# A two-layer adaLN block over 16 samples on one core: a new order of calls on every engine

## The reference

```
h = layernorm(x) * (1 + ca) + sa
x = x + ga * attention(h)                 # softmax((q k + q rel) / sqrt(8)) v, 16 heads
h = layernorm(x) * (1 + cb) + sb
x = x + gb * experts(h)                   # top 4 of 16, down((up + 1) * gate * sigmoid(1.702 gate))
# second layer, other weights
h = layernorm(x) * (1 + ca) + sa
k = exp(1j * 10 * (h @ Wk)); v = h @ Wv   # 1024 columns each
pos   = real(cumsum(v * rotors) * conj(rotors)) / sqrt(t)
assoc = real(cumsum(v * conj(shift(k))) * k)    / sqrt(t)
x = x + ga * ((pos * g0 + assoc * g1) @ Wo)
h = layernorm(x) * (1 + cb) + sb
x = x + gb * sigmoid(xr @ Wr) * (relu(xk @ Wk2)**2 @ Wv2)
```

## Time and profile before

| | |
|---|---|
| median of 3 runs | 1395.64 us (1394.96 to 1398.1) |
| the profiled execution, first to last instruction | 1390.0 us |
| mean granted TensorE clock | 0.994 |
| one steady step | 81.3 us |
| busy over the span | PE 90%, DVE 82%, ACT 70%, POOL 20% |
| DMA | 29.8 MB, mean 21 GB/s |

### The profile page before, as it was taken

How to read it: one execution, slowest core, us unless ns; L and a number is a source line. 1 busy time by engine, 2 the same in 40 slices (tenths; PEclk the granted TensorE clock), 3 DMA queues, 4 the chain that set the end, 5 groups by cost and what they waited for, 6 DMA issues and landing times.

```text
span 1390.0 us, 22686 instructions
## 1 busy us (share of the span) xinstructions
PE 1248.1 (90%) x7130; PEld 938.9 (68%) x7130; DVE 1136.3 (82%) x2104; ACT 970.5 (70%) x1699; POOL 280.8 (20%) x258
## 2 busy tenths in 40 slices
PE   7798998989899898989989898998989899898989
PEld 5475775758577575757758575775857577585778
DVE  7758879797987979798797979879797987979765
ACT  1665767778676777867677786767778676776841
POOL 4030221303022130302213031221303122130200
PEclk9899999999999999999999999999999999999999
DMA  5330301204030110403012030301204030120000
GB/s 126 93 35 5 35 9 16 20 8 34 8 34 8 15 19 8 34 8 32 10 13 21 8 34 8 31 10 13 21 8 34 8 31 11 12 22 5 1 4 4
DMA packets 54392, 29.82 MB, mean 21 GB/s; under 512 B 3725, under 2 KB 53338, under 8 KB 54362
## 3 DMA queue, kind: packets, MB, share of 16 engines
q1 hardware_dynamic: 52472, 28.74, 17.2%
q10 hardware_dynamic: 1890, 0.70, 0.5%
HBM read 8.20 MB, written 2.10 MB: 7 GB/s over the span
## 4 chain that ended last, share of the span: by engine, by line
PE 56%; DVE 14%; ACT 14%; issue 10%; POOL 2%; DMA 1%; SPq 1%; ACTq 1%; DVEq 0%; POOLq 0%
PE ring L762 15%; PE pb L862 7%; PE pa L776 7%; DVE smax L1814 5%; PE pa L680 4%; PE ring L667 3%; PE ring L716 3%; PE pb_k L792 2%; DVE prod L1927 2%; ACT prob L1279 2%; PE ring L749 2%; PE ring L629 2%; PE pb_v L820 1%; ACT L1383 1%; ACT frac L1386 1%
## 5 line engine op out<-in xcount | busy, mean ns | idle before, releaser
L427 POOL TENSOR_TENSOR gsc<-gsc,sc_all 128x512 f32<-128x512 f32 x128 | 175.7, 1377 | 353.2 <-ACT gsc L1344 353.2
L762 PE MATMUL ring<-ht,wgu 128*128 128x256 f32 x1024 | 241.5, 384 | 1.0 <-ACT sc_all L1332 1.0
L1954 DVE TENSOR_TENSOR_SCAN prod<-keep,prod 128x512 f32<-128x512 f32 x188 | 224.2, 1214 | 0.0
L762 PEld LDWEIGHTS ring<-ht,wgu 128*128 128x128 f32 x1024 | 193.2, 191 | 34.8 <-issue 5.0
L1814 DVE TENSOR_REDUCE smax<-ring 128x4 f32<-128x1024 f32 x128 | 153.3, 1219 | 17.6 <-PE ring L629 10.8
L1887 DVE SCALAR_TENSOR_TENSOR prob<-prob,gsc 128x512 f32<-128x512 f32 x120 | 81.4, 688 | 81.9 <-POOL gsc L427 63.5
L862 PE MATMUL pb<-prod,wo 128*128 128x256 f32 x544 | 129.3, 382 | 5.9 <-DVE prod L1968 5.8
L1279 ACT ACTIVATE prob<-ring 128x1024 f32<-128x1024 f32 x128 | 125.7, 1024 | 5.1 <-PE ring L667 3.5
L1339 ACT ACTIVATE gsc<-ring,gub_t 128x256 f32<-128x256 f32 x256 | 110.5, 501 | 21.3 <-PE ring L762 21.0
L776 PE MATMUL pa<-prob,wdown 128*128 128x256 f32 x512 | 122.0, 380 | 1.8 <-DVE prob L1881 1.8
L862 PEld LDWEIGHTS pb<-prod,wo 128*128 128x128 f32 x544 | 102.0, 190 | 25.2 <-DVE prod L1968 12.0
(11 more groups left out here) (284 smaller groups left out, 2476.1 us busy)
## 6 DMA issues: line engine op xcount, KB each, us to landing
q_rows<-qk_part SPq DMA_DIRECT2D x144, 64.0 KB
k_rows<-qk_part SPq DMA_DIRECT2D x135, 64.0 KB
x_in<-in_L_attn_x_dram SPq DMA_DIRECT2D x16, 128.0 KB, 2.1
sc_all<-_L_ffn_gate_up_proj_dram SPq DMA_DIRECT2D x1, 2048.0 KB, 11.9
out_dram<-xo SPq DMA_DIRECT2D x16, 128.0 KB, 1.8
prob<-in_L_wmod_dram SPq DMA_DIRECT2D x2, 384.0 KB, 3.9
k_rows<-qk_part ACTq DMA_DIRECT2D x9, 64.0 KB
wo<-in_L_attn_Wo_dram SPq DMA_DIRECT2D x1, 512.0 KB, 7.4
```

Source lines behind the costliest of these rows:

```text
L427: pool.tensor_tensor(gsc[:, n % NG, :], gsc[:, n % NG, :], sca, ALU.mult).then_inc(S["gsc"], 1)
L762: last = mm(ring[:, n % 2, g * 512 + j * L:g * 512 + (j + 1) * L], lhsT=wgu[:, 2 * n + j, g, :], rhs=ht[:, :], start=True, stop=True, skip ...
L1954: nc.vector.tensor_tensor_scan(prod[:, h, n - 1, :], keep[:, :], prod[:, h, n - 1, :], 0.0, ALU.mult, ALU.add).then_inc(S["cu" + str(n)], 1)
```

## The change

No operation is added to or taken from a steady step; each engine's list of calls in `step`, `first` and `last` is put in another order. Apart from order:

- on ACT `phase(b, 0)` leaves the start of the step and stands at its end as `phase(a, 0)` (it works on the sample that will be `b` in the next step); `first` gets one and `last` loses one;
- waits of the first and last sample that were calls of their own (`rows_landed`, `values_free`, `weights_loaded`, `tables_ready`, `weights_copied`) are now made inside the calls that need them, for sample 0 alone;
- `warm_last`, which gave PE ten constant products in the step that has no `nx`, is gone, and in `last` two of the `warm(4, ...)` stand elsewhere.

The diff of ACT's `step`, cut to the pieces that the text speaks of (those of PE and DVE are told by rows below):

```
             def step(a, b, nx):
...
                 if on_a:
                     exps(a, 4)
+                    exps(a, 5)
                     copy_values(a, 0)
-                    exps(a, 5)
-                if on_b:
-                    phase(b, 2)
-                if on_a:
                     exps(a, 6)
                     exps(a, 7)
+                if on_b:
+                    phase(b, 2)
+                if on_a:
                     copy_values(a, 1)
...
+                if on_b:
+                    tables(b, 3)
+                if on_a:
+                    second_norm_2(a)
+                if on_b:
+                    value(b, 3)
+                if on_a:
+                    route(a)
+                    copy_scores(a)
                 if on_x:
                     part(nx)
                 if on_a:
-                    second_norm_2(a)
-                if on_x:
-                    part_2(nx)
-                if on_b:
-                    value(b, 3)
-                if on_a:
-                    route(a)
-                if on_b:
-                    tables(b, 3)
-                if on_a:
-                    copy_scores(a)
                     copy_broadcast(a, 0)
                     copy_broadcast(a, 1)
                     copy_broadcast(a, 2)
+                if on_x:
+                    part_2(nx)
+                if on_a:
                     copy_broadcast(a, 3)
...
+                if on_a:
+                    phase(a, 0)
```

More of the change, by code:

```diff
@@ L72, with is_first, is_last @@
          "ang_1", "ang_2", "ang_3", "ang", "ang_abs") + tuple("tab%d" % n for n in range(8)) + ("wo_s", "wk_s"))
+def is_first(b):
+    return isinstance(b, int) and b == 0
+def is_last(b):
+    return isinstance(b, int) and b == LAST
 def scans(b):
-    return () if isinstance(b, int) and b == LAST else SCANS
+    return () if is_last(b) else SCANS
 def sums_done(b, c):
@@ L90, in sums @@
 def sums(b):
-    return () if isinstance(b, int) and b == LAST else SUMS
+    return () if is_last(b) else SUMS
 def build(nc, x, Wqkv, bqkv, Wout, bout, rel_emb, router_w, router_b, gup, gub, down, downb, c0, wmod0,
@@ L942, in step @@
                 if on_a:
+                    values(a, 3)
+                    scores_t(a, 6)
                     scores_t(a, 7)
@@ L963, in step @@
                 if on_a:
-                    mean(a, "2", x1[:, :], "x1", pa, ())
+                    variance(a, "2", pa, sq)
+                if on_b:
+                    phase_values(b, 3)
+                if on_a:
+                    deviation(a, "2", pa, rstd)
                 if on_x:
@@ L967, in step @@
                 if on_a:
-                    variance(a, "2", pa, sq)
+                    router(a)
+                    warm_scores(a, 2)
                 if on_b:
-                    time_values(b, 2)
-                if on_a:
-                    deviation(a, "2", pa, rstd)
-                if on_b:
-                    phase_values(b, 3)
-                if on_a:
-                    router(a)
+                    memory_wo(b, 1)
+                if on_x:
+                    head_6(nx)
                 if on_b:
@@ L989, in step @@
                 if on_a:
-                    broadcast(a, 2, nx)
-                if on_x:
-                    head_6(nx)
-                if on_a:
-                    broadcast(a, 3, nx)
+                    broadcast(a, 2)
+                    broadcast(a, 3)
+                    down_bias(a)
                     gate_up(a, 0)
                     gate_up(a, 1)
+                    gate_up(a, 2)
                 if on_b:
@@ L999, in step @@
                 if on_a:
-                    gate_up(a, 2)
-                    down_bias(a, nx)
                     gate_up(a, 3)
@@ L1004, in step @@
                     down_pair(a, 0)
+                    down_pair(a, 1)
                     gate_up(a, 5)
-                    down_pair(a, 1)
+                    gate_up(a, 6)
                     down_pair(a, 2)
-                    gate_up(a, 6)
                 if on_b:
@@ L1012, in step @@
                     gate_up(a, 7)
+                    down_pair(a, 3)
                 if on_b:
@@ L1015, in step @@
                 if on_a:
-                    down_pair(a, 3)
                     down_pair(a, 4)
-                if on_b:
-                    variance(b, "4", pb, sqb)
-                if on_a and on_x:
+                if on_x:
                     scores(nx, 0)
@@ L1023, in step @@
                 if on_b:
+                    variance(b, "4", pb, sqb)
+                if on_a:
+                    down_pair(a, 5)
+                if on_x:
+                    scores(nx, 2)
+                if on_b:
                     deviation(b, "4", pb, rstdb)
                 if on_a:
-                    down_pair(a, 5)
                     down_pair(a, 6)
@@ L2134, in step @@
                     expert_last(a, 6)
+                if on_x:
+                    maxima(nx, 0)
                 if on_b:
@@ L2137, in step @@
                 if on_x:
-                    maxima(nx, 0)
-                if on_b:
-                    scale(b, "4", centb, pb)
+                    maxima(nx, 1)
                 if on_a:
@@ L2143, in step @@
                 if on_b:
-                    mix_in(b)
+                    scale(b, "4", centb, pb)
+                if on_x:
+                    maxima(nx, 2)
                 if on_a:
                     experts_out(a)
-                if on_x:
-                    maxima(nx, 1)
+                if on_b:
+                    mix_in(b)
                 if on_a:
```

321 lines of the change are left out of this document (152 added, 169 removed).

## The result

| | before | after |
|---|---|---|
| median | 1395.62 us | 1441.31 us |
| lowest to highest of 4 runs each | 1394.96 to 1398.1 | 1431.15 to 1464.0 |
| ratio, 95% interval | | 1.030 (1.027 to 1.033), slower |
| profiled execution, span | 1390.0 us | 1462.3 us |

The change costs 3.0%; the forecast was 1392, and 1410 the end of its range. The profiled execution of the changed kernel is the longest of its four, so the pattern is read from it and not the median; its runs differ by 33 us where those of before differ by 3.

What follows compares the result with a forecast made beforehand. Bound: a relay of PE, DVE and ACT, time lying in hand-overs. Fourteen steps +1.4 us, step 15 -2.5, first -2, last -0.5: -3.6, so span 1390.0 becomes 1386.4, plus 5.6 for the median: 1392 us, range 1362 to 1410.

Steps and rivals of the forecast that it cites:

- P to E: From a step's first product of phases(b, 0) to the end of turn_scores: 38.9 us, about 1.2 earlier.
- Rival D: Before the end of turn_scores nothing is gained, DVE holding centre; step 1.2 us longer, 1409 us; chance 0.14.
- The issue: First DMA of the next sample's rows issued 7.3 us behind the end of turn_scores, 11.5 us later than before.
- PE's own work from E to L: Between turn_scores' end (E) and scores(nx, 0) (L), PE's work alone takes 27.7 us, against 29.3 before.
- The landing: Rows land 28.4 to 31.4 us behind turn_scores' end, middle 29.9; scores(nx, 0) waits 0.7 to 3.7 us.
- The clock: Behind the wait at scores(nx, 0), half rate for some 3 us in one step of three: 0.5 us a step.
- L to P: From scores(nx, 0) to the next step's first product of phases(b, 0): 12.0 us, 0.2 more than before.
- Rival B: The clock falls behind the rows' wait in every step, 1.6 us each; 1407 us, slower; chance 0.16.
- The first sample: In first, rows start some 4 us earlier but three down_pair stand behind the tiles: -2 us, between 0 and -4.
- Step 15 and last: Step 15 spreads nothing and gains 2.5 us; last and the missing warm_last give -0.5, between -2 and +2.
- the sum's own form: Per-step sum over front, rows' landing, score tiles and clock: -1.2 + 0.6 + 0.2 + 0.5 = +0.1 us.

Runs made afterwards that it cites:

- e4: Changed kernel with part straight ahead of route and part_2 straight behind route on ACT; 1401.47 us, ratio 1.0039 to the kernel before.
- e5: e4 with split_max of the steady step straight behind maxima(a, 7) again on DVE; 1387.35 us, ratio 0.9938 to the kernel before.
- e6: e5 with part_2 behind copy_scores instead of ahead of it; 1379.9 us, ratio 0.9879 to the kernel before.
- e2: Kernel before with only part moved behind copy_scores and part_2 ahead of copy_broadcast 3 on ACT; 1445.63 us, ratio 1.0338.
- e11: Changed kernel with 8 identity products on PE straight ahead of scores(nx, 0); 1438.97 us, ratio 1.0300 to the kernel before.

## Why the prediction was wrong

**P to E: right.** 38.9 was forecast and 39.13 to 39.14 measured in nine of thirteen steps, 39.39 in the mean. Rival D is out. What I had not seen is that the new front holds two waits in a row, 1.31 and 0.78 us, that can take the clock down; the changed kernel pays for that in three steps, e4 in all. The first of the two comes from a move that neither my account of the change nor my sum has: on DVE `split_max(a)` went behind `stats_and_mod(nx)` and `memory_a(b, 1)`.

**The issue: right.** E + 7.3 forecast, E + 7.5 in every step. Also right were the releaser of the new wait, its place and the unequal steps.

**PE's own work from E to L: 1.05 too short.** 27.7 forecast, 28.75 measured. I gave `down_bias` its new place at no cost; it waits 0.58 us there for values of DVE, and DVE has one of its products at 1.65 us (0.67 or 0.68 elsewhere) beside the first of POOL's moved subtractions. PE, DVE and POOL:

```profile
249.92 0.67 PE L776 MATMUL pa<-sct,dbias 16*128 16x256 f32 x2 [0.58 <-DVE vt L1805]
```

```profile
246.02 1.65 DVE L1958 TENSOR_TENSOR prod<-prod,sin_t 128x512 f32<-128x512 f32 x1
```

```profile
245.73 1.38 POOL L419 TENSOR_TENSOR qk<-qk,qk_part 128x512 f32<-128x512 f32 x1 [8.91 <-ACT qk_part L1253]
```

I had put no price on the two subtractions in their new place. It is half of the 1.05: in e5, where both subtractions lie ahead of these products, the same DVE product takes 0.68 us, `down_bias` does not wait, and E to L is 28.38 against 28.87 in e6, which has the 0.58 us again. PE and DVE of e5:

```profile
564.45 0.69 PE L776 MATMUL pa<-sct,dbias 16*128 16x256 f32 x2
```

```profile
561.20 0.68 DVE L1958 TENSOR_TENSOR prod<-prod,sin_t 128x512 f32<-128x512 f32 x1
```

The other half is in my count of PE's own work, and was not traced.

**The landing: the first step that failed.** I read from the stretches when the last bytes moved and took that for the moment at which PE can start. In the changed kernel PE's product comes 1.1 to 2.0 us behind the last stretch with bytes, 1.7 in the mean. In `first`, the only place in the trace of before where the rows were awaited, the two seemed to be 0.3 apart; there SP issues the load of x behind the spread, at 96.82, and it lands 10.7 us later, behind the start of the tiles at 107.30; so the last bytes were most likely those of x, and the 0.3 say nothing of the rows. One case was too little to read it from. The spreads themselves are little slower than before: last bytes 22.0 to 25.5 us behind the issue, mean 23.4, against 21.0 to 24.5, mean 22.8, in the thirteen steps of before, where I had used 22.6 as the middle. So L is at E + 32.6 in the mean instead of 29.9, beyond the late end of 31.4 in eight of thirteen steps, and the wait 3.84 instead of 2.2. The 2.7 are 0.2 (issue), 0.8 (transfers) and 1.7 (handing over).

The Trainium skill (DMA: Bandwidth & Descriptors, Anatomy of one DMA) puts most of a DMA's fixed cost of about 2 us behind the last byte, in the confirmation of the write ahead of the semaphore; it says so of another queue than SP's. The 1.1 to 2.0 us here agree with it, and it is what I should have added.

**The clock: the second.** I counted a fall of 3 us in one step of three, 0.5 us a step. It fell behind L in twelve of thirteen, and where the wait was over 3.3 us it lasted 6.8 or 10.2 us, not 3. L to P is 12.04 without a fall, as I had counted (12.0), 13.48 with the short one, 14.6 to 16.0 with the long ones: 2.3 us a step in the mean. The short one is the size that I had read from `first`, and my upper bound, 1.6 us in every step, was that size as well, although the wait it hangs on was beyond all that the steps had shown. A longer fall did stand in the trace of before, and I had not looked there: among the first sample's scores the clock is at 0.50 from 42.7 to 49.5 us, behind a wait of 1.40 us. PE, and two stretches of it:

```profile
43.72 1.08 PE L680 MATMUL pa<-prob,vt 128*32 128x256 f32 x8 [1.40 <-DVE mods L1675]
```

```profile
43.00:44.00 1.00, 0.28 (x4) 0.23 (x8) 0.93 (x4) 1.00 (x2) 0.00 (x0) 0.50 0.34 84
...
48.00:49.00 1.00, 1.00 (x10) 0.25 (x3) 1.00 (x1) 0.81 (x1) 0.00 (x0) 0.50 1.27 313
```

Rival B had the right mechanism (a fall in every step) at 1407, with both sizes too small.

**The first sample: wrong in sign.** -2 forecast, +4.2 measured. The rows did start 2.7 us earlier, but took 26.3 us to PE's hands instead of 22.5, and the three `down_pair`, which had stood ahead of the tiles and filled the time, ran behind the wait, at half the clock for the most part.

**Step 15 and last.** -2.0 (forecast -2.5) and +1.0 (forecast -0.5 within -2 to +2).

Put together with the sizes measured, the sum's own form gives -0.7 + 3.3 + 2.5 = +5.1 a step; the fourteen steps measured +69, first, step 15 and last +3.2. The other runs of the changed kernel are up to 33 us shorter; a spread that lands 3 us earlier saves its wait and the long fall behind it, so that small differences of the transfers are enlarged. How many of each kind these runs had was not profiled. Their mean granted clocks are 0.967 to 0.971 against 0.958; estimated from these, they spent 83 to 96 us at half clock and the profiled one 123, where the profiled one of before spent 17. So most of the loss at half clock is in them too.

## What to carry to other kernels

A transfer's slack is what lies between its issue and its first reader, less the transfer, less another 2 us for handing over: before moving a call that feeds a DMA, take all three from the trace, for the slowest transfer and not for the middle one. A wait of PE is to be priced with the clock behind it: look through the whole trace for the longest fall, and do not take the shortest for the upper bound; filling part of such a wait with products that wait for nothing is a cheap way to see that share apart. And a copy moved on one engine moves its successors on others: here POOL's subtraction, which beside a DVE operation on the critical chain cost 0.9 us.

## What the runs showed of the hardware

- **Handing over a DMA.** 1.1 to 2.0 us, read to a quarter of a microsecond, from the last moving bytes to the first product that waits for them, in the fourteen steps of the changed kernel.
- **The granted clock.** Behind L it falls for 3.4, 6.8 or 10.2 us. In the changed kernel waits of 2.3 to 3.1 us gave 3.4, and waits of 3.35 us and more gave 6.8 or 10.2; in e2 waits of 3.50 and 3.58 gave 3.4, so the length of the wait alone does not set it. Waits of 1.8 to 2.0 us gave both a fall and none, in e2 and in e11. Two waits of 1.1 to 1.3 and 0.8 us in a row gave no fall in the profiled execution of e5, three in thirteen steps in e6, and one in each of the thirteen in e4. What tips it was not settled.
- **DVE beside POOL.** An operation of 0.19 us took 1.13, a scan of 1.22 took 2.09, each to within 0.15 us as if it had started when POOL's subtraction ended; without the subtraction beside it the first was back at 0.19. The Trainium skill (SBUF — State Buffer, Who interferes with whom) says that a DVE instruction with two SBUF inputs and a GpSimd instruction that reads SBUF exclude each other for a whole instruction. These rows agree.
- **Equal spreads differ.** Issue to PE's hands is 23.2 to 24.6 or 26.2 to 27.0 us in the thirteen steps of the changed kernel, with the same bytes; in e2 it is also 22.0 and 25.3 to 25.4, so there are no two fixed kinds. SP's issues stretch with it: most take 0.61 us and the last few 1.0 to 1.9, and the last one ends 13.7 to 14.2 us behind the first in the six slow spreads and 12.7 to 13.4 in the other seven. Which is cause and which effect was not looked for.
